# Two levels of the seven-product scheme in a fused adaLN/FFN kernel, with W's operands kept in SBUF through a phase

## The reference

```python
y = x @ weight.T + bias1 + scale[b] * (x @ a_sel[b].T) @ b_sel[b].T
w = NF4[codes] * absmax            # one absmax per 64 values
out = x + y @ w.T + bias2
```

## Time and profile before

| What | Value |
|---|---|
| Median of three runs | 2213.49 us |
| Profiled execution, span from its first to its last instruction | 2211.8 us |
| PE busy | 2166.8 us, 98% |
| PE weight loads busy | 1859.8 us, 84% |
| DVE busy | 1790.3 us, 81% |
| ACT busy | 1016.5 us, 46% |
| POOL busy | 46.8 us, 2% |
| DMA | 558 MB, mean 252 GB/s |

### The profile page before, as it was taken

One profiled execution on the slowest core, in us unless ns is written; L12 is line 12 of the kernel. 1 busy time (PEld: TensorE's weight loads), 2 busy tenths in 40 slices (PEclk: granted clock), 3 DMA queues, 4 the chain that ended last, 5 costly groups with the idle time before them and its releaser, 6 DMA issues.

```text
span 2211.8 us, 31548 instructions
## 1 busy us (share of the span) xinstructions
PE 2166.8 (98%) x12104; PEld 1859.8 (84%) x12104; DVE 1790.3 (81%) x2647; ACT 1016.5 (46%) x1277; POOL 46.8 (2%) x55
## 2 busy tenths in 40 slices
PE   4899999999999999999999999999999999999999
PEld 4688788788878778899999988888988889888888
DVE  8899889768974664688778898888898887988887
ACT  8655555555553333444444443343443434443432
POOL 5100000000000000000000000000000000000000
PEclk8999999999999999999999999999999999999999
DMA  9688788887887897777777887777977877877775
GB/s 285 218 255 268 226 260 267 261 257 240 271 260 237 276 306 228 270 239 239 234 244 233 271 283 240 241 245 246 304 251 240 253 245 257 289 249 246 239 244 173
DMA packets 381172, 558.00 MB, mean 252 GB/s; under 512 B 23376, under 2 KB 234992, under 8 KB 380896
## 3 DMA queue, kind: packets, MB, share of 16 engines
q1 hardware_dynamic: 377712, 544.95, 77.6%
q0 software_dynamic: 3312, 11.03, 1.6%
HBM read 427.96 MB, written 128.99 MB: 252 GB/s over the span
## 4 chain that ended last, share of the span: by engine, by line
PE 91%; DVE 4%; DMA 3%; issue 1%; ACT 0%; SPq 0%; DVEq 0%; ACTq 0%
PE ps L1441 26%; PE ps L1273 14%; PE ps L1275 14%; PE ps L1274 14%; PE ps L1442 13%; PE ps L1445 4%; PE ps L1288 2%; PE ps L1444 2%; DMA rq<-xc_d 1%; PE ps L1321 1%; PE ps L1269 1%; DMA xc_d<-rq 1%; DMA xr<-xc_d 0%; DVE low_tw L966 0%; DVE tile L987 0%
## 5 line engine op out<-in xcount | busy, mean ns | idle before, releaser
L1441 PE MATMUL ps<-comb,xs 128*128 128x512 f32 x2527 | 903.3, 395 | 0.8 <-DVE comb L1047 0.8
L767 ACT CAST xs<-xr 128x1024 fp32r<-128x1024 f32 x427 | 448.3, 1051 | 629.8 <-DMA xr<-xc_d 628.9
L1442 PE MATMUL ps<-comb,xs 128*128 128x256 f32 x2527 | 707.8, 280 | 0.0
L1053 DVE TENSOR_TENSOR xs<-xr,xs 128x1024 fp32r<-128x1024 f32 x427 | 521.4, 1221 | 130.8 <-ACT xs L767 127.8
L1441 PEld LDWEIGHTS ps<-comb,xs 128*128 128x128 f32 x2527 | 474.3, 188 | 103.5 <-DVE comb L1047 1.1
L1442 PEld LDWEIGHTS ps<-comb,xs 128*128 128x128 f32 x2527 | 475.4, 188 | 14.5
L1273 PE MATMUL ps<-wq,tile 128*128 128x512 f32 x1088 | 468.2, 430 | 1.9 <-DVE tile L987 1.8
L1275 PE MATMUL ps<-wq,tile 128*128 128x512 f32 x1088 | 427.5, 393 | 0.0
L1274 PE MATMUL ps<-wq,tile 128*128 128x512 f32 x1088 | 426.1, 392 | 0.0
L1273 PEld LDWEIGHTS ps<-wq,tile 128*128 128x128 f32 x1088 | 205.2, 189 | 70.1 <-ACT cs L735 3.5
L1275 PEld LDWEIGHTS ps<-wq,tile 128*128 128x128 f32 x1088 | 204.9, 188 | 45.0
(11 more groups left out here) (119 smaller groups left out, 2219.8 us busy)
## 6 DMA issues: line engine op xcount, KB each, us to landing
xr<-xc_d SPq DMA_DIRECT2D x427, 512.0 KB, 4.0
raw<-in_L_cond_weight_dram SPq DMA_DIRECT2D x128, 512.0 KB, 4.8
xc_d<-rq SPq DMA_DIRECT2D x26, 1792.0 KB, 7.5
res<-in_x_dram SPq DMA_DIRECT2D x64, 512.0 KB, 5.2
out_dram<-res SPq DMA_DIRECT2D x128, 256.0 KB, 4.5
wc_d<-cs SPq DMA_DIRECT2D x32, 896.0 KB, 4.6
comb_raw<-wc_d SPq DMA_DIRECT2D x28, 1024.0 KB, 7.8
x_nat<-in_x_dram SPq DMA_DIRECT2D x104, 256.0 KB, 3.9
```

The costliest lines, as they stand in the source:

```text
L767: nc.scalar.copy(xs[f][:, HI, :, :], xr[f][:, LO, :, :]).then_inc(s_xhi, 1)
L1053: tt(xs[f][:, LO, :, :], xr[f][:, LO, :, :], xs[f][:, HI, :, :].bitcast(F32), ALU.subtract).then_inc(s_xlo, 1)
L1441: nc.tensor.matmul(bank[:, :], x_hi, both, start=(k == 0), stop=False)
L1442: nc.tensor.matmul(bank[:, 0:HW], x_lo, high, start=False, stop=False)
```

## The change

W is applied with two levels of the scheme. The first-level forms become seven phases (`PHASES`), each over all tokens: 8 groups (NT) of four token tiles. In a phase the form's W block (1024 x 1024) is again cut in four; its seven second-level operands (B11, T3, T1, T2, B21, B22, T4, each 4 k-steps by 512 columns) are loaded or made once and stay in SBUF (`wb`, eight slots of 16 KB per partition, one spare, rotated by `HOMES`). At a change of phase four blocks are loaded; DVE makes T1 and T2, GpSimd makes T3 and T4, ACT and DVE split all seven. For each group the first-level x forms are loaded (two blocks of 512 KB), DVE makes the four second-level sums (`x_block_sum`), and seven products of 4 k-steps of three matmuls of 512 columns follow, 392 products in all.

The later products of a group accumulate in the PSUM banks of the earlier ones; ACT copies P1 and P5 out, DVE makes u2 and u3 (`make_u`), and the output blocks are added on DVE (from PSUM) and GpSimd (from SBUF: `add_u`, `add_u3`). What a phase gives to the output goes through a buffer `o_sb` of DRAM sums `acc_d`: loaded (`load_addend`), added to, stored (`store_rows`). The last phase (it >= LAST) adds to two such buffers, the second of which (`e_sb`) lies in the spare W slot. The identity is added to W's diagonal blocks in the build, so that x itself is not loaded again for the residual. The low-rank part is accumulated in the first four phases by matmuls of 256 columns (`multiply_low`), restacked by float32 matmuls (`restack`), and multiplied by g in the last three phases; in the last one the difference of two low-rank parts is also multiplied.

In the build the order of the output rows and W tiles changes (row = (NS*u + j)*P, `PAIR_K`), each store of sums becomes two DMAs with runs of 128 elements, and the first phase's operands are loaded and split in the last tiles of the build, in slices of three k-steps and one (`FIRST_SPLITS`).

The core of the diff:

```diff
+    HH = HK // 2
+    NT = PAIRS // 2
+    PHASES = [A11, S2, S4, S3, A12, A22, SS1]
+    LOW_OF = [0, 1, 1, 2]
+    FINAL = NT * len(LOW_OF)
+    A_SLOTS = [(slice(8, 12), 0), (slice(1, 4, 2), 1), (slice(5, 8, 2), 2)]
+    LAST = NT * (NF - 1)
+    ITERS = NT * NF
+    PRODUCTS = NF * ITERS
...
+    B11, T3, T1, T2, B21, B22, T4 = range(7)
+    SPLIT_ORDER = [B11, T3, T1, B22, T2, B21, T4]
...
+    HOMES = [[0, 1, 2, 3, 5, 4, 6, 7]]
+    for _ in range(NF - 1):
+        b11, t3, t1, t2, b21, b22, t4, spare = HOMES[-1]
+        HOMES.append([b11, spare, t1, t2, b21, t3, b22, t4])
...
+    HI_LEAD, LO_LEAD = 5, 4
...
+            def load_addend(it, r):
+                ph, t = divmod(it, NT)
+                if it >= 2:
+                    sp.wait_ge(s_out[it % 2][r], 16 * (it // 2))
+                if ph:
+                    sp.dma_start(o_sb[it % 2][:, r, :, :].rearrange("p d o -> p (d o)"), acc_d[ADDEND[ph], t, r]
+                                 ).then_inc(s_add[it % 2][r], 16)
+                if ph == NF - 1:
+                    if it >= LAST + 2:
+                        sp.wait_ge(s_oext[it % 2][r], 16 * ((it - LAST) // 2))
+                    else:
+                        sp.wait_ge(s_prod, NF * LAST)
+                    sp.dma_start(e_sb[it % 2][:, r, :, :].rearrange("p d o -> p (d o)"), acc_d[U3, t, r]
+                                 ).then_inc(s_ext[it % 2][r], 16)
+
...
+            def w_t3(ph, ks=slice(0, HH)):
+                b12, b22 = wr[HOMES[ph][T3]][:, LO, ks, :], wr[HOMES[ph][B22]][:, LO, ks, :]
...
+                tt(b12, b22, b12, ALU.subtract).then_inc(s_t34, 1)
...
+                out_ap, b21, t2 = (wr[HOMES[ph][r]][:, LO, :, :] for r in (T4, B21, T2))
...
+                tt(out_ap, b21, t2, ALU.subtract).then_inc(s_t34, 1)
...
+            def add_u(it):
+                ph = it // NT
...
+                mid = o_sb[it % 2][:, :, :, :].rearrange("p r d o -> p (r d) o")[:, 1:3, :]
+                tt(mid, mid, u, ALU.add).then_inc(s_pu, 1)
+                if ph == NF - 1:
...
+                    mid = e_sb[it % 2][:, :, :, :].rearrange("p r d o -> p (r d) o")[:, 1:3, :]
+                    tt(mid, mid, u, ALU.add).then_inc(s_pu, 1)
...
+            def add_u3(it):
...
+                tt(y, y, p5_sb[:, :], ALU.add).then_inc(s_y, 1)
+                pool.wait_ge(s_y, it - NT + 1)
+                if ph == NF - 1:
+                    e22 = e_sb[it % 2][:, 1, 1, :]
+                    tt(e22, e22, y, ALU.add)
+                tt(o22, o22, y, ALU.add).then_inc(s_p22, 1)
...
+                if pos == 4:
+                    if ph:
+                        add_u(it)
+                    if t == NT - 1 and ph + 1 < NF:
+                        w_t3(ph + 1)
+                if pos == 5:
+                    add_u3(it)
+                if pos == 0 and t == 0 and ph:
+                    w_t4(ph)
...
+                if pos == 0:
+                    if it:
+                        store_rows(it - 1, 0)
+                if pos == 1 and it + 1 < ITERS:
+                    load_x(2 * it + 3)
+                if pos == 2:
+                    if it:
+                        store_rows(it - 1, 1)
+                    if it + 1 < ITERS:
+                        load_addend(it + 1, 0)
+                    if it + 2 < FINAL:
+                        load_a(it + 2)
+                if pos == 3 and it + 2 < ITERS:
+                    load_x(2 * it + 4)
+                if pos == 4 and it + 1 < ITERS:
+                    load_addend(it + 1, 1)
+                if ph + 1 < NF:
+                    if t == 3 and pos == 5:
+                        sp.wait_ge(s_prod, NF * NT * ph)
+                        if ph == 0:
+                            sp.wait_ge(s_wst, 32 * HK * NS)
+                        load_w(ph + 1, homes[7], 0, 1)
+                    if t == NT - 1 and pos == 1:
+                        sp.wait_ge(s_prod, n)
+                        load_w(ph + 1, homes[B11], 0, 0)
+                    if t == NT - 1 and pos == 2:
+                        sp.wait_ge(s_prod, n)
+                        load_w(ph + 1, homes[T3], 1, 1)
+                    if t == NT - 1 and pos == 5:
+                        sp.wait_ge(s_prod, n)
+                        load_w(ph + 1, homes[B21], 1, 0)
+                if it + 1 == FINAL and pos == 6:
+                    load_g(0)
+                if it >= FINAL:
+                    if pos == 1:
+                        load_g(2 * (it - FINAL) + 1)
...
+            def x_block_sum(it, role):
+                left, right = x_raw[2 * it % 3], x_raw[(2 * it + 1) % 3]
+                a11, a12, a21, a22 = left[:, 0], left[:, 1], right[:, 0], right[:, 1]
...
+                if role == T3:
...
+                    ins = tt(xr[role][:, LO], a11, a21, ALU.subtract)
+                elif role == T1:
+                    ins = tt(xr[role][:, LO], a21, a22, ALU.add)
...
+            for n in range(PRODUCTS):
+                it, pos = divmod(n, NF)
+                ph, t = divmod(it, NT)
+                if pos == 0 and it:
+                    block21(it - 1)
+                    if it > LAST:
+                        second11(it - 1)
+                        second22(it - 1)
+                if pos == 1 and it > LAST:
+                    second12(it - 1)
+                if pos == 2 and it > LAST:
+                    second21(it - 1)
+                if pos == 4:
+                    make_u(it)
+                if it + 1 < ITERS and pos in (T3 + 1, T1 + 1, T2 + 1, B22 + 1):
+                    x_block_sum(it + 1, pos - 1)
+                if pos == 5 and ph:
+                    block11(it)
+                if pos == 6:
+                    block12(it)
+                    if it >= FINAL:
+                        block22(it)
+                if n + LO_LEAD < PRODUCTS:
+                    x_lo(n + LO_LEAD)
+                if pos == 5 and it < FINAL:
+                    sum_low(it)
+                if pos == 5 and it + 1 < FINAL:
...
+                if t == NT - 1 and ph + 1 < NF:
+                    if pos == 3:
+                        w_t1(ph + 1)
+                    if pos == 4:
+                        w_lo(ph + 1, B11)
+                    if pos == 5:
+                        w_t2(ph + 1)
+                        w_lo(ph + 1, T3)
+                    if pos == 6:
+                        w_lo(ph + 1, T1)
+                if t == 0 and ph:
+                    if pos == 0:
+                        w_lo(ph, B22)
+                    if pos == 1:
+                        w_lo(ph, T2)
+                    if pos == 2:
+                        w_lo(ph, B21)
+                    if pos == 3:
+                        w_lo(ph, T4)
...
+                final, two = it >= FINAL, it >= LAST
+                if t == 0:
+                    pe.wait_ge(s_wlo, splits_before(ph, pos))
+                pe.wait_ge(s_xlo, n + 1)
+                if it < FINAL and pos in (B11, T3, T2, B21):
...
+                        pe.wait_ge(s_low, 2 * it)
+                    if final:
...
+                    pe.wait_ge(s_u1, it + 1)
...
+                    pe.wait_ge(s_u3, it + 1)
+                bank, home, fresh = group[pos][it % 2][:, :], wb[HOMES[ph][pos]], pos < B21
+                for k in range(HH):
+                    last = three(bank, xs[pos][:, HI, k, :], xs[pos][:, LO, k, :], home[:, HI, k, :], home[:, LO, k, :],
+                                 fresh and k == 0, k == HH - 1, onto=not fresh)
+                if final and pos == B21:
+                    pe.wait_ge(s_gblo, 2 * (it - FINAL) + 2)
...
+                if final and pos == T4:
+                    last = lora(it, bank_c, 1, 0)
...
+                    pe.wait_ge(s_u2, it + 1)
+                    lora(it, bank_b, 1, 1, start=True).then_inc(s_l22, 1)
+                if two and pos == T4:
+                    pe.wait_ge(s_o11, 2 * it + 1 - LAST)
+                    difference(it, bank_a, 0, 0)
+                    pe.wait_ge(s_o22, 2 * it + 1 - LAST - FINAL)
+                    difference(it, bank_b, 1, 1)
+                if it > LAST and pos == B11:
+                    pe.wait_ge(s_o12, 2 * it - 1 - LAST)
+                    difference(it - 1, bank_d, 0, 1)
+                if it > LAST and pos == T3:
+                    pe.wait_ge(s_o21, 2 * it - 1 - LAST)
+                    difference(it - 1, bank_c, 1, 0)
+                if final and pos == T3:
+                    restack(it)
+            pe.wait_ge(s_o12, 2 * ITERS - 1 - LAST)
+            difference(ITERS - 1, bank_d, 0, 1)
+            pe.wait_ge(s_o21, 2 * ITERS - 1 - LAST)
```

1110 lines of the change are left out of this document (625 added, 485 removed).

## The result

The changed kernel takes 2323.08 us (median of four runs, 2320.2 to 2326.04) against 2212.76 for the kernel before on the same chip: ratio 1.05, 95% interval 1.0485 to 1.0515. I had forecast slower, but 2236 us, with a range to 2298. 87 us are missing from the sum.

What follows compares the result with a forecast made beforehand. Applying W was taken as paced by TensorE's matmul spacing, VectorE next; 1186 + 8 + 70 + 20 + 35 + 10 = 1329 us against 1309.3, tail +2, gave a median of 2236 us, range 2150 to 2298.

Steps and rivals of the forecast that it cites:

- build's stores: Building W: stores split in two with 512-byte runs; PE never waits for them, costed at nothing.
- start of the first phase: From build to applying: first product 4 us late, the fourth 6, from VectorE's W parts and a DRAM round trip: 10 us.
- five changes: Changes of W operands between phases: PE waits for VectorE's and GpSimd's work on W, 14 us each, 70 us.
- last change: Change before the last phase: W loads queue behind SyncE's wait for a result buffer, then sums and splits follow: 20 us.
- last phase: Two output buffers: PE waits 3.2 us for the 22 block and 1.2 behind the x load, 4.4 x 8 = 35 us.
- steady iterations: From the second phase on, A's low parts come late behind GpSimd: 0.4 us in each of 21 iterations, 8 us.
- The matmuls: Apply stage: 392 products of twelve 512-column matmuls at 0.227 us; PE's work 1186 us in all, 123 less than before.
- Rival (d): Apply stage: strided x tiles or accumulating into used banks space matmuls wider than 0.227 us, at 0.235: 2274 us; chance 0.08.
- GpSimd excludes VectorE: Apply stage, the forecast's own case: GpSimd holds VectorE for its own duration; 2236 us, own range 2210 to 2260; chance 0.45.
- rival (b): Apply stage: GpSimd's sums fall beside PSUM reads and idle time, so exclusion hardly tells; 2163 us; chance 0.33.
- Rival (c): Apply stage: each 1024 elements of GpSimd cost VectorE 3.2 us; 2305 us; chance 0.14.

Runs made afterwards that it cites:

- the fills: Changed kernel with each GpSimd sum in the apply stage replaced by two memsets of the same output, sums left out: 2201.54 us, ratio 0.995 to before.
- the best kernel with nothing left out: Changed kernel with GpSimd's W and block sums on VectorE, first phase's included, W halves adjacent in DRAM, loads and low parts reordered: 2219.53 us, ratio 1.0027.

## Why the prediction was wrong

**Direction right, mechanism right, sizes too small.** The range to 2298 was missed by 25 us. Excess over PE's work, in us, as the sum had it and as the trace of the kernel after shows it:

| term | predicted | measured |
|---|---|---|
| build's stores | 0 | 16 |
| start of the first phase | 10 | 20 |
| five changes | 70 (14 each) | 109 (21.8 each) |
| last change | 20 | 34 |
| last phase | 35 (4.4 in each of eight iterations) | 53 (8.5 in each of the six behind the last change, 2 in the last) |
| steady iterations | 8 | 4 |

The differences are 16 + 10 + 39 + 14 + 18 - 4 = 93 us, against 87 missing; PE's own iterations (32 x 21.0 + 16 x 20.4 + 8 x 22.8 = 1181) were 5 us cheaper than the 1186 of the sum.

- **The matmuls** held. 0.227 us spacing, 21.0 us for a steady iteration where 20.9 were predicted. Rival (d) had nothing to it.
- **GpSimd excludes VectorE** held, and rival (b) fell: with the reads taken away the changes cost 8.3, not 21.8. Rival (c) names 2305, the nearest figure, but not for its reason: in the kernel after no VectorE operation was held for longer than GpSimd's lasted. The price is what failed: I charged GpSimd 9 us of a change's 14; the fills say 13.5. The durations were scaled for GpSimd alone, and there they were right: 1.27 us at least for 512 elements where I had 1.3, 4.6 for 2048 where I had 4.5. But beside VectorE they were 1.7 in the mean, and 5.6 (T3) and 6.3 (T4): GpSimd is held by VectorE in turn, so both columns of the account grow.
- **The phase change is the step that failed most.** "From position 3 of the last iteration to the fourth operand's readiness DVE has ... 26 us, where PE is there after 20.9" stops at the fourth operand, as if PE never waited behind it. Counted as the sum counts it, from position 3 to the product of the fourth operand, PE was late by 17.7 us in the mean of the five (13.5 to 23.0), against 16 worked out and 14 taken; with the fills by 6.2, against 5. The other 4.1 of the 21.8 us lie behind the fourth operand: at the change at 1292, a wait of 2.8 us at the next iteration's start, which ends as VectorE ends the A operand's low parts, and 1.7 us of slow products. Over the two iterations VectorE has 13.3 us each of ordinary work, and 20 to 24 us for W. "5 us of stall with GpSimd free of charge" measured 8.3 with fills in the whole change, and 15 to 16 with the sums on VectorE.
- **The start** has the same cause as far as it shows: 20 us for 10, with the fills 11.
- **The last phase**: I had both of its waits. The one for the 22 block was 2.5 us where I had 3.2. The store ahead of the x load I named too, but let it cost 1.2 us. It held PE for 2.8 us in an iteration, and 5.7 us with what followed. Moving one DMA issue was worth 34 us.
- **The last change**: the queue of the two loads was given 5.5 us; moving them gained 3.5. The fills bring the change to 20.8, so GpSimd's part is 13 us here too; VectorE is not busy throughout (47.7 of 60 us), and the rest was not taken apart.
- **"In the build PE never waits for them and I cost these at nothing"** failed. I named the evacuation as the cover that might go. It was not that store, but the x store beside it that became slow, and through it a chain of three transfers that had no room (PE already waited 0.5 us for it at 200 us in the trace before). I looked at the size of runs, not at where they go.
- **The clock**, which the sum did not have at all, looked like the missing term and was not, at the changes: filled, it came back and the time stayed. A lower clock cost nothing while PE had to wait for VectorE anyhow. In the last phase it seems to have cost over 2 us an iteration.

None of these repairs made the change win: with VectorE as the main bound of each change, the best kernel with nothing left out is 2219.5 us, 0.27% slower than before. Six changes of operands, each with 20 to 24 us of work on the engine that has 7.7 us of room per iteration, still cost 100 of the 123 us that the products save, and the start 17.

## What to carry to other kernels

When work is given to GpSimd to relieve VectorE, count it on VectorE as well wherever both read SBUF and VectorE's instruction has two inputs there: here the relief of some 400 us cost more than doing the sums on VectorE. At a change of resident operands, add up each engine's whole work until the steady state is back, not until the first operands are ready. And before a slow clock or an idle time is made the culprit, fill it: if the time does not move, look whose rows did not move either; that engine owns it.

## What was not expected of the hardware

- GpSimd's memset beside VectorE is free for VectorE: 0.684 us for its two-input operations, where a GpSimd sum made them 1.20 (low parts, mean) and 2.31 (the x sum).
- A VectorE instruction of 512 elements and one of 1536 both lasted 5.1 us for the same reason, so a mean of a line tells little: for 512 elements 0.68 is the minimum, and the longest was 5.10, beside a GpSimd sum of 5.07.
- 512-byte runs to two places 1 MB apart made another queue entry's 1 MB store land in 8.4 instead of 5.5 us; 512-byte runs to neighbouring places cost the whole kernel 0.1% (and that store landed in 6.0 instead of 5.3).
- Two DMA issues exchanged in one queue, 2.6 us apart, cost 69 us.
